# Loads in held-back groups, and a first walk through TensorE's code, in a two-block convolution kernel

## The chip, the cores and the metric

The kernel runs on one core of a Trainium2 chip. The metric is the device time of one execution in microseconds. Times in this text are in us unless marked otherwise. TensorE is the matrix engine (PE in the rows; PEld its weight loads), VectorE is DVE, ScalarE is ACT, GpSimd is POOL and SyncE is SP. A q behind an engine's name in a row (SPq) means its sequencer: DMA issues, branches, waits.

## The reference

The input x has 16 images of 32 channels with 128 x 128 pixels in float32. Two residual blocks follow each other:

```
x = x + conv3x3(group_norm(x, 16 groups), masked L0 weights)
x = x + conv5x5(group_norm(x, 16 groups), L1 weights) + bias
```

The 3x3 weights are masked by a threshold on the mean of their absolute values. The reference writes the 5x5 convolution with Fourier transforms; it equals a direct one with padding 2. A group is two channels of one image, so each normalization needs the mean and variance of whole images.

## The kernel before, in words

**Halves and steps.** Each image is worked on in two halves of 64 rows, 32 halves in all (h). A half is held in two layouts. In x_bands and mid_bands the partitions are 4 bands x 32 channels, each band 16 rows with a halo above and below: this is what the matmuls read. In x_own and mid they are 4 interleaved sets of rows x 32 channels, as the results come out of the matmuls. Float32 accuracy comes from splitting: values and weights are each a float16 high part and a float16 low part, and three of the four products are taken (high x high, high x low, low x high).

**Stages of a half.** load_bands(h) brings x in bands (4 DMAs of 272 to 288 KB), load_own(h) the same rows in the other layout (4 DMAs of 256 KB). VectorE takes statistics of the bands (stats_in, L635). When both halves of an image are done, they are combined over the partitions: for images 0 and 1 of x and image 0 of mid by a small matmul on TensorE (mix_members, L948, and combine on VectorE), later by a round trip through DRAM (spread_stats and gather_stats on ScalarE, group_stats on VectorE). Then scale_of, normalize3 (L709 or ScalarE's L449), high3 (L404, x_hi), low3 (L737, x_lo), the 3x3 convolution on TensorE, take_conv3 (L757: adds x_own and makes mid; its drain at L760 frees the PSUM banks, bank3_go), stats_out (L765), and move_mid(h): 16 DMAs (L273) that bring mid into bands, with move_edges (L280, L284) for the halo rows between halves. The 5x5 convolution of a half comes LAG = 3 steps later, then take_conv5 (L481), the addition on GpSimd (L380) and store_out.

**TensorE's program.** In the lead (halves 0 to 2) a small piece of code, lead_conv, does one 3x3 convolution at a time, with some matmuls on constant data (keep_warm) between. From step 3 on, a loop does in each step the 3x3 convolution of half s and the 5x5 convolution of half s - 3: whole_step (pairs3_high, pairs3_low), conv5 (pairs5_high), conv3_rest (singles3), conv5_rest (singles5, pairs5_low), with a branch at L1004 back to whole_step, which a prefetch hint at L990 goes with. In a step there are 144 + 320 + 144 + 240 + 160 = 1008 matmuls, each with its weight load. whole_step is aligned to 256 instructions. The program starts with a branch (L959) to lead_start, which lies behind lead_conv; there it waits for mix_members(("x", 0)).

**Queues and order.** SyncE issues nearly all DMAs, in program order, in one queue: bands 0, 1 and 2, w5, bands 3, own 0 and 1; then it waits for mid_made (the first take_conv3) and goes on with own 2, move 0, an edge, bands 4, own 3, an edge, bands 5, move 2, bands 6 and 7. Nothing holds one load back until another has landed; SyncE stops only at these waits, or where the queue is full. GpSimd issues move 1 (16 DMAs), with its two operations on w5 (L371 and L374) between them. VectorE's order in the lead is written out by hand (L785 to L833):

```
stats_in(0..1), set_apart(x 0), drain, combine(x 0), scale_of(x 0), normalize3(0), low3(0),
stats_in(2..3), set_apart(x 1), largest(w5), take_conv3(0), low3(1), combine(x 1), scale_of(x 1),
stats_out(0), take_conv3(1), low3(2), over_partitions, power_of_two, undo_power (scale of w5),
stats_out(1), set_apart(mid 0), take_conv3(2), ...
stats_in(6), stats_in(7), group_stats(x 2), scale_of(x 2), normalize3(4), take_conv3(3), ..., low3(4)
```

## Time and profile before

| what | value |
|---|---|
| median of 3 runs | 806.02 us (805.27 to 806.18) |
| the profiled execution | 805.87 us |
| its span | 804.1 us |
| TensorE busy | 748.7 us, 93% |
| VectorE busy | 611.8 us, 76% |
| mean granted TensorE clock | 0.988 |
| DMA | 150.49 MB, mean 187 GB/s |

The profile is of one execution. The span is the time from the first to the last instruction of the core; 1.8 us lie around it. Busy times are the union of an engine's instructions. The share of the DMA engines in the view of stretches is the mean over 16 engines and can exceed 1, as packets on one engine overlap. The idle time in front of an instruction is put down to what ended it; "issue" means nothing that the profile shows. Queue q1 is SyncE's loads and stores; q8 and q14 carry instructions, q8 in packets of 16 KB.

### The profile page before, as it was taken

The page shows a single profiled execution, that of the slowest core. Times are in us where ns is not written, and L with a number is a line of the kernel's source. Part 1 is how long each engine was busy: PE and PEld are TensorE (multiplying, and loading weights), DVE is VectorE, ACT ScalarE, POOL GpSimd, SP SyncE. Part 2 cuts the span into 40 slices and gives each one's busy share as a digit, 9 for nine tenths or more (in the row PEclk, how much of TensorE's full clock was granted, in tenths as well). Part 3 has the DMA queues.
Part 4 walks back from the last instruction along what each step waited for, and adds up shares of the span by engine and source line. Part 5 has one row for each costly group of instructions (what it writes and reads, how often), then busy time and mean ns, then how long its engine had stood idle before and what let it go on. Part 6 is the DMA issues. An engine that isn't in the chain of part 4 may idle for free.

```text
span 804.1 us, 67794 instructions
## 1 busy us (share of the span) xinstructions
PE 748.7 (93%) x32292; PEld 552.8 (69%) x32292; DVE 611.8 (76%) x959; ACT 332.4 (41%) x287; POOL 267.9 (33%) x161
## 2 busy tenths in 40 slices
PE   0786699999999999999999999999999999999996
PEld 0443367777787777877777787777778777776564
DVE  5897598797878788787878788797878796664541
ACT  0351235363534435363444435363444426362410
POOL 1050044432324343432234343422234343322360
PEclk9998999999999999999999999999999999999999
DMA  8999589999998979798998979898998957573424
GB/s 196 194 202 218 130 173 230 222 224 216 228 203 213 221 169 223 180 220 198 229 203 194 229 165 230 183 225 197 225 210 205 199 126 165 133 167 86 103 52 104
DMA packets 234176, 150.49 MB, mean 187 GB/s; under 512 B 18656, under 2 KB 227616, under 8 KB 230048
## 3 DMA queue, kind: packets, MB, share of 16 engines
q1 hardware_dynamic: 227168, 144.00, 81.8%
q10 hardware_dynamic: 6272, 4.90, 2.5%
q0 software_dynamic: 704, 1.25, 0.7%
q14 instruction: 22, 0.18, 0.1%
q8 instruction: 10, 0.16, 0.1%
HBM read 75.60 MB, written 33.59 MB: 136 GB/s over the span
## 4 chain that ended last, share of the span: by engine, by line
PE 86%; DVE 5%; SPq 3%; DMA 3%; issue 1%; DVEq 1%; ACT 1%; ACTq 0%
PE psum L887 66%; PE psum L904 21%; DMA x_bands<-x_dram 3%; SPq L265 1%; SPq L273 1%; DVE bn_in L635 1%; DVE x_lo L737 1%; DVE bn_out L765 1%; DVE mid L757 1%; DVEq L760 1%; SPq L280 0%; ACT conv_out L481 0%; ACT x_hi L411 0%; DVE x_bands L709 0%; DVE mid L868 0%
## 5 line engine op out<-in xcount | busy, mean ns | idle before, releaser
L380 POOL TENSOR_TENSOR mid<-mid,conv_out 128x512 f32<-128x512 f32 x118 | 244.6, 2103 | 471.1 <-ACT conv_out L481 471.1
L887 PE MATMUL psum<-x_hi,s_hi 32*64 32x508 f16 (+2 forms) x6656 | 200.2, 381 | 13.2 <-ACTq L521 4.8
L887 PE MATMUL psum<-x_lo,s_hi 32*64 32x508 f16 (+2 forms) x6656 | 197.6, 379 | 3.8 <-DVE x_lo L737 2.8
L887 PE MATMUL psum<-x_hi,s_lo 32*64 32x508 f16 (+2 forms) x6656 | 198.1, 377 | 0.6 <-issue 0.6
L887 PEld LDWEIGHTS psum<-x_hi,s_hi 32*64 32x64 f16 x6656 | 130.4, 105 | 70.8 <-issue 9.5
L887 PEld LDWEIGHTS psum<-x_hi,s_lo 32*64 32x64 f16 x6656 | 149.7, 104 | 36.3 <-issue 3.5
L887 PEld LDWEIGHTS psum<-x_lo,s_hi 32*64 32x64 f16 x6656 | 108.5, 104 | 78.4 <-issue 9.8
L757 DVE SCALAR_TENSOR_TENSOR mid<-psum,unscale,x_own 128x1024 f32<-128x1024 f32 x64 | 79.2, 1278 | 93.2 <-PE psum L904 93.1
L404 ACT ACTIVATE x_hi<-x_bands 128x2304 f16<-128x2304 f32 x31 | 65.7, 2118 | 116.0 <-PE psum L904 116.0
L481 ACT ACTIVATE conv_out<-psum,bias,unscale 128x512 f32<-128x512 f32 x118 | 82.3, 776 | 60.1 <-PE psum L887 58.7
L745 DVE TENSOR_TENSOR x_lo<-mid_bands,x_hi 128x2560 f16<-128x2560 f32 x32 | 93.5, 2921 | 2.9 <-PE psum L887 2.8
L442 ACT ACTIVATE x_hi<-mid_bands 128x2560 f16<-128x2560 f32 x31 | 72.5, 2338 | 49.9 <-PE psum L904 48.4
L397 ACT ACTIVATE root<-gvar 128x1 f32<-128x1 f32 x32 | 6.5, 203 | 194.0 <-DVE gvar L688 168.7
L635 DVE BATCH_NORM_STATS2 bn_in<-x_bands 128x6 f32<-128x512 f32 x128 | 76.9, 664 | 12.1 <-DMA x_bands<-x_dram 12.1
L449 ACT ACTIVATE mid_bands<-mid_bands,nbias,gscale 128x2560 f32<-128x2560 f32 x31 | 78.2, 2524 | 15.8 <-DVE nbias L702 13.3
L765 DVE BATCH_NORM_STATS2 bn_out<-mid 128x6 f32<-128x512 f32 x128 | 79.1, 681 | 4.4 <-DVE mid L757 0.5
L737 DVE TENSOR_TENSOR x_lo<-x_bands,x_hi 128x2304 f16<-128x2304 f32 x32 | 80.7, 2523 | 1.5 <-ACT x_hi L415 1.1
L904 PE MATMUL psum<-x_hi,s_hi 32*32 32x508 f16 (+2 forms) x4096 | 74.0, 377 | 6.2 <-issue 6.2
L904 PE MATMUL psum<-x_hi,s_lo 32*32 32x508 f16 (+2 forms) x4096 | 73.9, 378 | 0.0
L904 PEld LDWEIGHTS psum<-x_hi,s_hi 32*32 32x32 f16 x4096 | 53.2, 88 | 24.2 <-issue 20.0
L709 DVE TENSOR_SCALAR x_bands<-x_bands,gmean,gscale 128x2304 f32<-128x2304 f32 x29 | 68.8, 2373 | 0.0
L904 PE MATMUL psum<-x_lo,s_hi 32*32 32x508 f16 (+2 forms) x4096 | 67.1, 381 | 0.8 <-issue 0.8
(88 smaller groups left out, 342.6 us busy)
## 6 DMA issues: line engine op xcount, KB each, us to landing
x_own<-x_dram SPq DMA_DIRECT2D x128, 256.0 KB, 4.9
mid_bands<-mid SPq DMA_DIRECT2D x372, 80.0 KB
out_dram<-mid SPq DMA_DIRECT2D x112, 256.0 KB, 5.4
x_bands<-x_dram SPq DMA_DIRECT2D x96, 288.0 KB, 6.0
x_bands<-x_dram SPq DMA_DIRECT2D x32, 272.0 KB, 6.6
mid_bands<-mid SPq DMA_DIRECT2D x124, 64.0 KB
every_mv<-mv_scratch ACTq DMA_DIRECT2D x16, 256.0 KB, 3.9
out_dram<-mid SPq DMA_DIRECT2D x28, 128.0 KB, 2.4
```

The source lines that it names most:

```text
L380: nc.gpsimd.tensor_tensor(m, m, conv_out[:, b, :], ALU.add).then_inc(out_added, 1)
L442: nc.scalar.activation(x5_hi[:, :, 2:2 + W], mid_bands[:, k % MB_SLOTS, :, :], ACT.Copy).then_inc(hi5_done, 1)
L449: nc.scalar.activation(v, v, ACT.Identity, bias=nbias[:, at], scale=gscale[:, at]).then_inc(act_scaled, 1)
L481: nc.scalar.activation(conv_out[:, b, :], psum[:, X5_BANK + b, :], ACT.Identity, bias=bias[:, 0:1], scale=unscale[:, 1:2]).then_inc(conv5_ ...
L635: nc.vector.bn_stats(bn_in[:, h // 2 % 2, h % 2, b, :], rows.rearrange("p a w -> p (a w)")).then_inc(bn_x, 1)
L709: nc.vector.tensor_scalar(v, x_bands[:, h % XB_SLOTS, :, :], gmean[:, 0:1], gscale[:, 0:1], ALU.subtract, ALU.mult).then_inc(scaled, 1)
L737: nc.vector.tensor_tensor(x3_lo[:, :, 2:2 + W], x_bands[:, h % XB_SLOTS if h else SPARE, :, :], x3_hi[:, :, 2:2 + W], ALU.subtract).then_i ...
L745: nc.vector.tensor_tensor(x5_lo[:, :, 2:2 + W], mid_bands[:, k % MB_SLOTS, :, :], x5_hi[:, :, 2:2 + W], ALU.subtract).then_inc(x5_lo_go, 1)
L757: nc.vector.scalar_tensor_tensor(mid[:, h % MID_SLOTS, at, :], psum[:, X3_BANK + at.start:X3_BANK + at.stop, :], unscale[:, 0:1], x_own[:, ...
L765: nc.vector.bn_stats(bn_out[:, h % 2, b, :], mid[:, h % MID_SLOTS, b, :]).then_inc(bn_mid, 1)
L887: ins = nc.tensor.matmul(psum[2 * C * J:2 * C * (J + 1), bank + i, :].rearrange("p (a w) -> p a w", a=A)[:, :, c0:c1], w[quad(i), at:at + ...
L904: ins = nc.tensor.matmul(psum[quad(j), bank + i, :].rearrange("p (a w) -> p a w", a=A)[:, :, c0:c1], w[quad(i), at, :], src[quad(i), j + d ...
```

## The change

Four things change.

1. load_own and load_bands take a semaphore and a count. With them, the group's first DMA is issued, and the other three only when that semaphore says that the group before has landed. It is used from the second group on for all loads of the lead up to bands 7. w5 is loaded before bands 2 instead of behind them.
2. VectorE takes the largest of w5 before combine(("x", 0)), and computes its scale between normalize3(0) and low3(0).
3. GpSimd does its two operations on w5 before move 1, and ScalarE makes s5_hi (high_w5) behind high3(1) instead of high3(3).
4. TensorE's program starts with a branch to fetch_second, and from there to fetch_third and fetch_fourth. Each of these stubs is a nop and a branch, and lies between parts of the loop's code: behind whole_step, behind the first half of pairs5_high, and within its second half. The fourth branch goes to lead_start. The parts of the loop are joined by three branches (whole_step to conv5, conv5 to conv5_more, conv5_more to conv5_last); their matmuls and their order are the same.

The diff, cut to its core:

```diff
         @block.sync
-            def load_own(h):
+            def load_own(h, behind=None, count=0):
                 for j in range(Q):
+                    if behind is not None and j == 1:
+                        sp.wait_ge(behind, 16 * count)
                     sp.dma_start(as_rows(x_own, j, h % X_SLOTS), own_rows(x[h // 2], h % 2, j),
                                  ).then_inc(x_own_in[h % X_SLOTS], 16)
...
             load_bands(0)
-            load_bands(1)
-            load_bands(2)
+            load_bands(1, x_bands_in[0], Q)
             for q in range(Q):
                 sp.dma_start(w5[quad(q), :, :], w5_dram.rearrange("i a b o -> i (a b) o")).then_inc(w_loaded, 16)
-            load_bands(3)
-            load_own(0)
-            load_own(1)
+            load_bands(2, x_bands_in[1], Q)
+            load_bands(3, x_bands_in[2], Q)
+            load_own(0, x_bands_in[3], Q)
+            load_own(1, x_own_in[0], Q)
             sp.wait_ge(mid_made, PIECES)
-            load_own(2)
+            load_own(2, x_own_in[1], Q)
             move_mid(0)
             move_edges(0, 1, 0)
-            load_bands(4)
-            load_own(3)
+            load_bands(4, mid_bands_in[0], MOVES)
+            load_own(3, x_bands_in[4], Q)
             move_edges(0, 0, 1)
-            load_bands(5)
+            load_bands(5, x_own_in[1], 2 * Q)
             move_mid(2)
-            load_bands(6)
-            load_bands(7)
+            load_bands(6, mid_bands_in[2], Q * Q)
+            load_bands(7, x_bands_in[0], 2 * Q)
...
         @block.gpsimd
+            pool.wait_ge(w5_bounded, 1)
+            nc.gpsimd.tensor_scalar(w5[:, :, :], w5[:, :, :], wfac[:, 1:2], None, ALU.mult).then_inc(w5_scaled, 1)
+            pool.wait_ge(w5_hi_made, 1)
+            nc.gpsimd.tensor_tensor(s5_lo[:, :, :], w5[:, :, :], s5_hi[:, :, :], ALU.subtract).then_inc(w5_split, 1)
             pool.wait_ge(mid_made, PIECES * 2)
...
         @block.vector
             set_apart("x", 0)
+            dve.wait_ge(w_loaded, 16 * Q)
+            largest(w5, 1)
             dve.drain().then_inc(bank3_go, 1)
...
             normalize3(0)
+            over_partitions(total[:, 1:2], bound[:, 1:2])
+            power_of_two(1)
+            undo_power(1)
             low3(0)
+            nc.vector.drain().then_inc(w5_bounded, 1)
...
         @block.tensor
-            pe.br("lead_start")
+            pe.br("fetch_second")
...
             with nc.body("whole_step", valid_engines=only):
                 hint = pe.mark_branch_hint_location()
                 pairs3_high()
                 pairs3_low()
+                pe.br("conv5")
+            with nc.body("fetch_second", valid_engines=only):
+                pe.nop().then_inc(code_touched, 1)
+                pe.br("fetch_third")
             with nc.body("conv5", valid_engines=only):
-                pairs5_high()
+                pe.wait_ge(x5_hi_go, 1)
+                pairs(s5_hi, x5_hi, K5, X5_BANK, start=True, every=x5_hi_go)
+                pe.br("conv5_more")
+            with nc.body("fetch_third", valid_engines=only):
+                pe.nop().then_inc(code_touched, 1)
+                pe.br("fetch_fourth")
+            with nc.body("conv5_more", valid_engines=only):
+                pairs(s5_lo, x5_hi, K5, X5_BANK, part=slice(0, 3))
+                pe.br("conv5_last")
+            with nc.body("fetch_fourth", valid_engines=only):
+                pe.nop().then_inc(code_touched, 1)
+                pe.br("lead_start")
+            with nc.body("conv5_last", valid_engines=only):
+                pairs(s5_lo, x5_hi, K5, X5_BANK, part=slice(3, K5))
                 pe.br_lt(step, HALVES, on_true="conv3_rest", on_false="conv5_rest")
```

## Rows read from the trace of the kernel before

**Rows 1.** The page, part 4: the chain that ended last, by engine.
```profile
PE 86%; DVE 5%; SPq 3%; DMA 3%; issue 1%; DVEq 1%; ACT 1%; ACTq 0%
```

**Rows 2.** Stretches: length; busy (count) by engine; TensorE's clock; DMA share; GB/s.
```profile
110.00:795.00 685.00, 679.80 (x30112) 514.20 (x30104) 525.38 (x786) 299.38 (x259) 246.02 (x118) 1.00 0.85 188
...
2.00:36.00 34.00, 12.64 (x310) 7.24 (x310) 24.08 (x62) 9.05 (x8) 2.47 (x10) 1.00 1.05 216
36.00:38.00 2.00, 0.50 (x16) 0.27 (x24) 1.80 (x3) 0.00 (x0) 0.00 (x0) 0.73 0.10 18
...
50.00:90.00 40.00, 26.77 (x834) 14.23 (x819) 28.08 (x54) 6.43 (x6) 11.75 (x16) 0.85 1.06 218
```

**Rows 3.** The chain in order of time, 80 to 107: start, length, what.
```profile
80.00 0.42 SPq L265
...
80.47 10.50 DMA x_bands<-x_dram
...
90.99 2.48 DVE bn_in L635 x4
...
96.39 1.48 DVE x_bands L709
...
99.27 1.20 DVEq L760
...
103.71 2.42 DVE x_lo L737
```

**Rows 4.** Waits up to 110: total, times, longest.
```profile
PE psum L904 <- issue: 7.0, 3, 4.8
...
PE psum L887 <- issue: 4.8, 3, 3.2
```

**Rows 5.** Timeline of TensorE and ScalarE: start, length, instruction, [idle before].
```profile
64.55 2.79 PE L887 MATMUL psum<-x_lo,s_hi 32*64 32x512 f16 x48 [2.38 <-DVE x_lo L737]
...
73.79 2.55 PE L887 MATMUL psum<-x_hi,s_hi 32*64 32x504 f16 x51 [3.16 <-issue]
...
98.27 2.12 ACT L404 ACTIVATE x_hi<-x_bands 128x2304 f16<-128x2304 f32 x1
...
102.75 1.67 PE L887 MATMUL psum<-x_hi,s_hi 32*64 32x512 f16 x48
...
106.18 1.53 PE L887 MATMUL psum<-x_lo,s_hi 32*64 32x512 f16 x48 [0.43 <-DVE x_lo L737]
```

**Rows 6.** Line 959; queue q8 in the 0.1 us from 1.8, 9.0 and 70.8.
```profile
L959 PEldq COMPARE_BRANCH  x1: 3695/3695/3695, 0.9 to 0.9; - x1
...
q8 instruction: 1, 0.02, 78.3%
...
q8 instruction: 1, 0.02, 77.4%
...
q8 instruction: 1, 0.02, 83.8%
```

**Rows 7.** Timeline of TensorE and VectorE, 20 to 37.
```profile
20.02 0.58 PE L948 MATMUL psum<-apart,mix_in 128*128 128x16 f32 x2 [20.02 <-DVE apart L657]
...
20.64 0.17 DVE L663 COPY members<-psum 128x16 f32<-128x16 f32 x1 [0.76 <-PE psum L948]
...
25.88 2.56 DVE L737 TENSOR_TENSOR x_lo<-x_bands,x_hi 128x2304 f16<-128x2304 f32 x1 [1.07 <-ACT x_hi L415]
...
33.91 0.98 DVE L586 TENSOR_REDUCE bound<-w 128x1 f32<-128x800 f32 x1
...
34.92 2.48 DVE L757 SCALAR_TENSOR_TENSOR mid<-psum,unscale,x_own 128x1024 f32<-128x1024 f32 x2
```

**Rows 8.** DMA issues of 5.9 to 6.2 and 30.3 to 30.8; SyncE's timeline.
```profile
x_bands<-x_dram SPq DMA_DIRECT2D x1, 272.0 KB, 10.7
...
x_own<-x_dram SPq DMA_DIRECT2D x2, 256.0 KB, 7.1
...
37.43 1.91 SPq L254 DMA_DIRECT2D x_own<-x_dram  x4
39.38 10.43 SPq L273 DMA_DIRECT2D mid_bands<-mid  x16
```

**Rows 9.** VectorE's timeline: first and last of the eight steps of w5's scale.
```profile
50.51 0.17 DVE L579 COPY across<-bound 128x32 f32<-128x32 f32 x1
...
51.94 0.15 DVE L601 TENSOR_SCALAR unscale<-power 128x1 f32<-128x1 f32 x1
```

**Rows 10.** Line 1004, the loop's branch: duration in ns, min/median/max.
```profile
L1004 PEldq COMPARE_BRANCH  x32: 71/217/240, 102.2 to 795.7; - x32
```

More of the change, by code:

```diff
@@ L148, in two_blocks @@
         apart_go = sem("apart_go")
+        code_touched = sem("code_touched")
         c3_whole = sem("c3_whole")
@@ L260, in store_out, with load_bands @@
                                  as_rows(mid, j, k % MID_SLOTS, banks)).then_inc(out_stored[k % MID_SLOTS], 16)
-            def load_bands(h):
+            def load_bands(h, behind=None, count=0):
                 for i in range(Q):
+                    if behind is not None and i == 1:
+                        sp.wait_ge(behind, 16 * count)
                     y0, y1, at = band(h % 2, i, 1)
@@ L368, in _ @@
                     pool.dma_start(to, rows).then_inc(mid1_moved, 16)
-                if i == 1:
-                    pool.wait_ge(w5_bounded, 1)
-                    nc.gpsimd.tensor_scalar(w5[:, :, :], w5[:, :, :], wfac[:, 1:2], None, ALU.mult).then_inc(w5_scaled, 1)
-                elif i == 2:
-                    pool.wait_ge(w5_hi_made, 1)
-                    nc.gpsimd.tensor_tensor(s5_lo[:, :, :], w5[:, :, :], s5_hi[:, :, :], ALU.subtract).then_inc(w5_split, 1)
             def add_out(k, b):
@@ L529, in _ @@
                     high3(1)
+                    high_w5()
                     take_root(("x", 1))
@@ L536, in _ @@
                     high3(3)
-                    high_w5()
                     take_root(("mid", 0))
@@ L797, in _ @@
             set_apart("x", 1)
-            dve.wait_ge(w_loaded, 16 * Q)
-            largest(w5, 1)
             take_conv3(0)
@@ L806, in _ @@
             low3(2)
-            over_partitions(total[:, 1:2], bound[:, 1:2])
-            power_of_two(1)
-            undo_power(1)
-            nc.vector.drain().then_inc(w5_bounded, 1)
             stats_out(1)
@@ L872, in _, with columns, pairs @@
         def _(pe):
-            def columns(k):
-                for dx in sorted(range(k), key=lambda d: abs(d - k // 2)):
+            def columns(k, part=slice(None)):
+                for dx in sorted(range(k), key=lambda d: abs(d - k // 2))[part]:
                     x0 = 2 - k // 2 + dx
                     yield dx, x0, max(0, 2 - x0), min(W, W + 2 - x0)
-            def pairs(w, src, k, bank, start=False, every=None):
-                for dx, x0, c0, c1 in columns(k):
+            def pairs(w, src, k, bank, start=False, every=None, part=slice(None)):
+                for dx, x0, c0, c1 in columns(k, part):
                     for dy in range(1, k):
@@ L926, in singles3 @@
                 singles(s3_hi, x3_lo, K3, X3_BANK).then_inc(c3_whole, 1)
-            def pairs5_high():
-                pe.wait_ge(x5_hi_go, 1)
-                pairs(s5_hi, x5_hi, K5, X5_BANK, start=True, every=x5_hi_go)
-                pairs(s5_lo, x5_hi, K5, X5_BANK)
             def singles5():
@@ L985, in _ @@
                 pe.br("lead_end")
-            nc.switch_bb("lead_end")
-            pe.addr_align(256, offset=0, max_nops=0)
-            pe.br("whole_step")
+            with nc.body("lead_end", valid_engines=only):
+                pe.addr_align(256, offset=0, max_nops=0)
+                pe.br("whole_step")
             with nc.body("whole_step", valid_engines=only):
```

## The prediction

> **What bounds the kernel now.** I read the page's chain first, for the engine that sets the end: TensorE [rows 1]. The view of stretches then says where time can be won. From 110 to 795 us TensorE is busy for 679.8 of 685 us [rows 2], so nothing can be gained there, and whatever happens in the lead (the first 106 us) is carried to the end one for one. In the lead the DMA engines are the full resource: 216 GB/s from 2 to 36 us and 218 GB/s from 50 to 90 us, their share above 1 in both [rows 2].
>
> The chain over the end of the lead [rows 3] is what the change has to beat. The last piece of load_bands(7), issued at 80.47, lands at 90.97. VectorE takes its statistics until 93.46, and only then, its program being in order, the group statistics of image 2, normalize3(4) at 96.39, take_conv3(3), stats_out(3) and low3(4), which ends at 106.13. TensorE begins pairs3_low(4) at 106.18, after 0.43 us of waiting for it [rows 5].
>
> Next the waits. TensorE loses 4.8 + 7.0 = 11.8 us before L887 and L904 to "issue" in this time [rows 4], all of it in its first pass over whole_step to conv5_rest, between 70 and 100 us. The instruction queue explains them: one q8 packet between 70.8 and 70.9, and TensorE goes on at 73.79 [rows 5, 6]. TensorE is fetching code that it has not yet run.
>
> **The change, part by part.** (a) *Code fetched ahead.* In whole_step and the bodies after it are 1008 matmuls with their loads (2016 instructions) and some ten others. The stubs touch its second to fourth parts. They take away the first of the stalls, at most the 11.8 us. But if step 3 ended 11.8 us sooner (before it ends at 102.75 [rows 5]), TensorE would stand before step 4: its x_hi, made by high3(4) behind the same statistics, comes at 98.27 + 2.12 = 100.4 [rows 5], bank3_go, the end of the drain at L760, at 100.47 and x_lo at 106.13 [rows 3]. The gain is 0.43 us, the wait now left, and not 11.8. What ends last there is the transfer of bands 7.
>
> The Trainium skill speaks against this part too (Runtime: NRT & Kernel Launch, "Instruction fetch mechanics": the instruction memory is a FIFO, "only 2 cache lines", and a taken branch outside it forces a fetch). By that rule the stubs' blocks would be gone before their use, and every jump back of the loop would fetch. The trace disagrees for TensorE: the branch that closes the loop, L1004, runs 32 times at a median of 0.217 us and at most 0.240 [rows 10], where a fetch cost 3.70 [rows 6]. So I count the stubs' blocks as kept; as (a) is worth 0.43 us at most, the sum is the same by either.
>
> (b) *What the stubs cost.* One jump to code that is not there takes 3.70 us, from 0.90 to 4.60, with nearly empty queues: 0.95 us to the packet at 1.85, and 2.75 from there to running [rows 6] (2.94 at 70.85 [rows 5, 6]). On arrival the next block is asked for; that packet starts only at 9.05, 4.45 us later, since the loads are under way by then [rows 6]. After the change TensorE needs four such trips in a row before lead_start instead of one. First to 4.60. Second: packet at 9.05, running at 11.8. Third: the packet starts between 0.95 and 4.45 us after 11.8, running at 15.5 to 19.0. Fourth, back to lead_start: 19.2 to 26.2, and if it stands behind the packet of the block after the fourth stub, up to some 28. I take delays near the loaded one for both, 3.8 and 4.0, as the rest of bands 1 and then w5 fill the queues at just that time: third at 18.3, lead_start at 25.0. It is needed at 20.02, for the mix of x 0 [rows 7]. **TensorE is 5.0 us late**, bounds 0 and 8. Behind that mix waits combine(("x", 0)) on VectorE (20.64, idle only 0.76 before it [rows 7]) and with it everything. A late mix gives nothing back: VectorE's queue is full until take_conv3(0) at 34.92.
>
> (c) *w5's work on VectorE.* largest (0.98 us [rows 7]) moves to before combine(x 0), where the wait of (b) covers it; without that cover it costs 0.3. It waits for w5, which now stands before bands 2: 0.4 MB at 216 GB/s behind bands 1 (16.6) land near 18.5 to 19, not late. The scale's eight small steps (50.51 to 52.09 [rows 9]: 1.6 us) go between normalize3(0) and low3(0). There VectorE was idle for 1.07 us [rows 7], so 0.6 us lie on the path. largest's old place before take_conv3(0) gives 0.98 back. Sum -0.3 on the path to take_conv3(0). The steps leave the path to take_conv3(2), which comes 1 to 2.5 us earlier; nothing that ends last hangs on it, as SyncE is still issuing older work when bands 6 and 7 are due. GpSimd's two w5 operations now go ahead of move 1, and its 16 moves without gaps; hidden.
>
> (d) *Held-back loads to take_conv3(0).* Each group's first DMA goes, and the rest waits until the group before has landed. From the landing to the first bytes of the rest pass an issue (0.42 us [rows 3]) and a start-up, which I set equal to the 0.95 us of (b): about 1.4 us. The DMA already queued covers 288 KB / 216 GB/s = 1.35 us of it, less where the 16 engines end apart: a pause of 0 to 0.6 us for each change of group. Bands 1's last DMA (issued 5.91, 10.7 us later landed [rows 8]) comes 0 to 0.6 later, own 1 (its last DMA is issued at 30.4, 7.1 to its landing: 37.5 [rows 8]) about 1 later. That is before the end of the new take_conv3(0), so own 1 costs nothing when TensorE is late; if it is not, about 0.5. Behind each waiting DMA on SyncE stand only the later loads, and, until mid_made, no move.
>
> So take_conv3(0) ends 5.0 - 0.3 = 4.7 later, and SyncE's wait for mid_made, behind which all later loads stand, too.
>
> (e) *Held-back loads from there to bands 7.* Before: SyncE goes on at 37.43 [rows 8], so 90.97 - 37.4 = 53.6 us. After, counted from that point: own 2 and move 0 as before (16 issues in 10.43 us [rows 8], set by SyncE), edges until 13.7. Bands 4's rest waits for the edges to land (15.3), then 1.2 start-up, 3 x 1.35 for itself and 2.2 for the moves of GpSimd beside it, 0.5 to the last landing: 23. Own 3's rest likewise 28.6 (no moves beside it), bands 5's 34.5. Move 2 is issued until 30.0 + 10.4 = 40.4 and has landed near 42.2; bands 6 near 48.1; bands 7's rest, behind which SyncE holds nothing urgent, 48.2 + 1.4 + 4.05 + 0.5 = 54.2. Until bands 7, what waits behind each held load on SyncE is the next of these, and the edges 0 to 1 and move 2, which nobody misses before step 4. **+0.6 us**, bounds -4.4 and +4. The lower bound is the 49.2 us that the bytes of own 2 and 3, bands 4 to 7 and three moves take with no pause (their DMAs at 1.2, 1.35 and 0.35 us each), the upper one four bare pauses of 1 us. The skill gives a fixed 2 us for each DMA (DMA: Bandwidth & Descriptors, "Anatomy of one DMA"), most of it after the last byte; by it each of four groups would pause for 2.0 - 1.35 = 0.65, together 2.6 instead of 0.6, and the sum would be 813.8.
>
> (f) *Clock.* TensorE will now stand idle for some microseconds before step 4. After 2.38 us of idle time its next 48 matmuls took 2.79 us instead of 1.53 [rows 5], the level of 1.2 GHz. pairs3_high(4) is then slow but hidden by the wait for x_lo; pairs3_low(4) may be slow: 0 or 1.3, I take 0.6.
>
> (g) *Three more branches in every step.* L1004 costs 0.217 us in the sequencer and the matmuls around it keep their pace [rows 5, 10]: they are queued ahead. Nothing; 0.1 us each if the cover were gone, 29 x 3 x 0.1 = 8.7.
>
> Sum: 4.7 + 0.6 + 0.6 - 0 = **+5.9 us**. The profiled execution took 805.87 us (span 804.1), the median is 806.02: 811.8 us.
>
> **The rivals.**
> *No late start, slower by little.* The held-back groups leave the queues emptier, the trips take 3.7 us each, lead_start is reached at 19.2. For it: the first trip. Against: the second, with only seven band loads issued (after: five). Left are (c) 0.3, (d) 0.5, (e) 0.6, (f) 0.6: 808.0.
> *Faster.* Short queues let each transfer run without a pause, and take the place of SyncE's long stalls in a full queue; bands 7 land 4.4 us sooner, with no late start. For it: there are pauses now, e.g. 36 to 38 us. Against: 218 GB/s over 40 us leave little. It decides if the packet of the third trip starts by 13.5 us and bands 7 land before 89: 806.0 - 4.4 + 1.0 = 802.6.
> *No difference.* Half of either: 806.
> *The branches are not hidden*: 811.8 + 8.7 = 820.5.
>
> **How the numbers follow.** Forecast 0.53 (own range 808.5 to 815.5, a TensorE late by 2 to 8 us); little slower 0.18, of which 0.10 over 0.2%; no difference 0.10; faster 0.14; branches 0.05. A measurement of this kernel tells 0.2%, 1.6 us. Faster 0.14, same 0.18, slower 0.68. The range leaves out the branches and most of faster: 804 to 817.
>
> **What would show it.** TensorE's first matmul (L948) at 25 instead of 20.02, and its branch instructions before it at 3 to 7 us each. Four q8 packets or more before 25 us. take_conv3(0) at 39.6 instead of 34.92. The stalls at 73.79, 79.73 and 87.90 gone, a wait for normalize3(4)'s or bank3_go's chain of 6 us or more in their place before step 4. Bands 7 landed near 96. From step 5 on steps as long as before. I am wrong if L948 stays at 20 (step (b)), if bands 7 land earlier than 90 ((e)), or if steady steps are longer ((g)).

## The result and the profile after

The changed kernel takes 817.97 us (median of 5, 816.34 to 820.3), the kernel before 805.97 us beside it (5, 805.23 to 806.18). The ratio is 1.0142, interval 1.0127 to 1.0158: slower by 12.0 us. The profiled execution took 816.34 us with a span of 814.5, 10.4 more than before. It is the shortest of the five, so the trace accounts for 10.4 us and leaves some 1.5 us of the medians' difference unseen. Of the runs further down, one execution of f2 took 1129.72 us at a mean granted clock of 0.657, where all others have 0.97 to 0.99; it is left out of the ratio, and without it the median of f2 is 807.09.

First the chain that ended last, by engine, from the page of the profile; [rows 1] has it for the kernel before.

```profile
PE 84%; DMA 8%; SPq 4%; DVE 2%; issue 1%; ACT 0%; DVEq 0%; ACTq 0%
```

The DMA engines' part of the chain went from 3% to 8%. The view of stretches says where the time is lost. A row has the stretch, its length, the busy time (and count) of the five engines, TensorE's granted clock, the DMA share and GB/s.

```profile
2.00:36.00 34.00, 12.52 (x304) 6.62 (x304) 23.35 (x66) 8.42 (x8) 4.76 (x11) 1.00 0.84 193
50.00:90.00 40.00, 32.03 (x1181) 19.30 (x1166) 24.48 (x42) 7.58 (x6) 8.93 (x16) 0.87 0.82 180
...
73.10:85.30 12.20, 8.36 (x416) 5.80 (x416) 5.17 (x9) 0.00 (x0) 0.00 (x0) 0.87 0.75 153
...
110.00:795.00 685.00, 678.59 (x29848) 496.36 (x29856) 535.85 (x795) 305.57 (x265) 251.56 (x119) 1.00 0.85 188
```

Behind the lead nothing changed: from the end of x_lo(4) to the end of the span are 697.7 us, before 698.0. In the lead, where [rows 2] had 216 and 218 GB/s, there are now 193 and 180, and in the 12.2 us from 73.1 on only 153 (the stretch in which SyncE issues move 2). The chain in order of time shows what the DMA engines wait for (start, length, what).

```profile
17.01 0.31 SPq L270
...
17.83 6.85 DMA x_bands<-x_dram
...
24.69 0.31 SPq L270
...
25.51 5.22 DMA x_bands<-x_dram
...
31.67 4.97 DMA x_own<-x_dram
...
37.55 4.80 DMA x_own<-x_dram
...
42.36 0.31 SPq L257
...
60.23 5.41 DMA x_bands<-x_dram
...
66.56 5.20 DMA x_own<-x_dram
...
90.18 5.40 DMA x_bands<-x_dram
...
96.42 5.30 DMA x_bands<-x_dram
101.74 2.47 DVE bn_in L639 x4
...
107.04 1.48 DVE x_bands L713
...
114.36 2.42 DVE x_lo L741
```

It is one pattern again and again: a group of loads lands, SyncE issues the rest of the next group (0.8 us from the landing to the end of the second issue), that group lands, and so on. Own 1 has landed at 42.35 instead of 37.52, bands 7 at 101.72 instead of 90.97, and x_lo(4) ends at 116.78 instead of 106.13. SyncE's timeline has the step between these (its first issue of each kind, the time that the group of issues takes, and their number):

```profile
42.36 1.38 SPq L257 DMA_DIRECT2D x_own<-x_dram  x3
43.79 10.63 SPq L278 DMA_DIRECT2D mid_bands<-mid  x16
...
60.70 6.35 SPq L257 DMA_DIRECT2D x_own<-x_dram  x4
...
68.28 4.75 SPq L270 DMA_DIRECT2D x_bands<-x_dram  x4
73.08 12.23 SPq L278 DMA_DIRECT2D mid_bands<-mid  x16
```

take_conv3(0) ended at 39.45, and SyncE then issued the first DMA of own 2; but own 2's second DMA waits for own 1, so that SyncE gets no further until 42.36. In the kernel before it went on at 37.43 [rows 8]. Move 2 is issued from 73.08; in the kernel before, SyncE came to it at 63.40:

```profile
60.43 2.93 SPq L265 DMA_DIRECT2D x_bands<-x_dram  x4
63.40 12.27 SPq L273 DMA_DIRECT2D mid_bands<-mid  x16
```

TensorE's branches in the lead, by line (duration in ns, min/median/max, first and last start), and its timeline:

```profile
L957 PEldq COMPARE_BRANCH  x1: 3810/3810/3810, 0.9 to 0.9; - x1
...
L994 PEldq COMPARE_BRANCH  x1: 6294/6294/6294, 4.9 to 4.9; - x1
...
L1002 PEldq COMPARE_BRANCH  x1: 4847/4847/4847, 11.4 to 11.4; - x1
...
L1008 PEldq COMPARE_BRANCH  x1: 5566/5566/5566, 16.6 to 16.6; - x1
...
L1019 PEldq COMPARE_BRANCH  x32: 82/228/3673, 93.7 to 806.1; - x32
```

```profile
22.28 0.58 PE L946 MATMUL psum<-apart,mix_in 128*128 128x16 f32 x2 [22.28 <-issue]
...
80.94 1.07 PE L908 MATMUL psum<-x_lo,s_hi 32*32 32x508 f16 x56 [2.53 <-issue]
...
84.97 0.62 PE L908 MATMUL psum<-x_hi,s_hi 32*32 32x504 f16 x8 [1.31 <-issue]
...
91.04 3.63 PE L891 MATMUL psum<-x_lo,s_hi 32*64 32x508 f16 x121 [1.50 <-issue]
111.22 2.79 PE L891 MATMUL psum<-x_hi,s_hi 32*64 32x512 f16 x48 [16.56 <-DVEq L764]
...
116.83 1.53 PE L891 MATMUL psum<-x_lo,s_hi 32*64 32x512 f16 x48 [0.37 <-DVE x_lo L741]
```

The four trips through the stubs took 20.5 us in all. The first mix comes 2.26 us later than in [rows 7]. Of the 11.8 us of stalls "issue" of [rows 4], 5.3 us are left (the three rows from 80.94 to 91.04), and in their place stand 16.56 us before step 4.

### The profile page after: what moved, and what is told of

Read it like the earlier page. It is cut to its first block, busy times and chain, and to the rows that moved or that the text cites. A ratio compares the mean times of both kernels' runs of the same rounds, so it can differ in the third digit from the quotient of the medians.

```text
span 814.5 us, 67893 instructions
## 1 busy us (share of the span) xinstructions
PE 749.9 (92%) x32292; PEld 537.9 (66%) x32292; DVE 610.6 (75%) x959; ACT 332.4 (41%) x287; POOL 268.5 (33%) x161
## 4 chain that ended last, share of the span: by engine, by line
PE 84%; DMA 8%; SPq 4%; DVE 2%; issue 1%; ACT 0%; DVEq 0%; ACTq 0%
PE psum L891 64%; PE psum L908 20%; DMA x_bands<-x_dram 5%; SPq L278 3%; DMA x_own<-x_dram 2%; DMA mid_bands<-mid 1%; SPq L270 1%; SPq L257 0%; DVE bn_out L769 0%; DVE bn_in L639 0%; DVE x_lo L741 0%; ACT conv_out L485 0%; DVE x_bands L713 0%; DVE mid L872 0%; DVEq L764 0%
## 5 line engine op out<-in xcount | busy, mean ns | idle before, releaser
L891 PEld LDWEIGHTS psum<-x_hi,s_hi 32*64 32x64 f16 x6656 | 124.4, 105 | 88.2 <-DVEq L764 21.8
L891 PEld LDWEIGHTS psum<-x_hi,s_lo 32*64 32x64 f16 x6656 | 141.7, 104 | 42.6 <-issue 1.4
L891 PEld LDWEIGHTS psum<-x_lo,s_hi 32*64 32x64 f16 x6656 | 107.0, 104 | 80.9 <-issue 10.4
```

The costliest lines, as they stand in the source:

```text
L891: ins = nc.tensor.matmul(psum[2 * C * J:2 * C * (J + 1), bank + i, :].rearrange("p (a w) -> p a w", a=A)[:, :, c0:c1], w[quad(i), at:at + ...
```

## The experiments

Go-on is the time from which SyncE is free to go on with own 2: mid_made, or own 1's landing where own 2 is held for it and that is later. Two lengths then describe every run's lead: from go-on to the first issue of move 2, and from there to the landing of bands 7. "Early waits" are those of bands 1 to own 1, "late waits" those from own 2 on.

| kernel | median us (runs) | ratio, interval | go-on | move 2 issued | bands 7 landed | x_lo(4) ends |
|---|---|---|---|---|---|---|
| before | 805.97 (5) | 1 | 37.4 | 63.40 | 90.97 | 106.12 |
| after | 817.97 (5) | 1.0142, 1.0127 to 1.0158 | 42.36 | 73.08 | 101.72 | 116.78 |
| e1_stubs_only | 817.2 (4) | 1.0128, 1.0111 to 1.0146 | 48.30 | 73.79 | 102.32 | 117.39 |
| e2_held_only | 815.83 (4) | 1.0109, 1.0092 to 1.0127 | 40.87 | 72.95 | 103.72 | 118.77 |
| e3_no_stubs | 817.43 (4) | 1.0138, 1.0118 to 1.0158 | 41.09 | 72.73 | 102.32 | 117.37 |
| e4_no_hold | 815.98 (4) | 1.0115, 1.0098 to 1.0132 | 47.23 | 73.83 | 101.37 | 116.59 |
| e5_two_ahead | 815.29 (4) | 1.0116, 1.0099 to 1.0132 | 39.84 | 71.08 | 98.82 | 113.88 |
| e6_hold_early | 808.65 (6) | 1.0041, 1.0022 to 1.0059 | 40.18 | 66.41 | 92.25 | 107.32 |
| e7_late_hold_no_stubs | 814.55 (4) | 1.0093, 1.007 to 1.0117 | 37.25 | 70.40 | 101.30 | 116.35 |
| e8_no_move_hold | 816.38 (4) | 1.0131, 1.011 to 1.0153 | 43.37 | 74.03 | 102.11 | 117.17 |
| f1_hold_before_move2 | 812.68 (5) | 1.0083, 1.007 to 1.0096 | 37.09 | 70.87 | 98.45 | 113.52 |
| f2_hold_bands7 | 807.18 (12) | 1.0015, 1.0005 to 1.0025 | 38.76 | 64.47 | 95.69 | 110.78 |

Times in the last four columns are of one profiled execution each, ratios of all. The profiled executions of e2 and f2 lie 2.4 and 2.6 us above their medians, those of e5 and e6 2.2 and 1.4 below. Without late waits before move 2, from go-on to move 2 are 25.5 to 26.6 us (before, e1, e4, e6, f2); with them 30.7 to 33.8 (after, e2, e3, e5, e7, e8, f1). From move 2 to bands 7 are 25.8 to 31.2 in all.

**Stubs and waits apart.** The first two put each half of the change into the kernel before, the next two take each out of the kernel after.

e1: the kernel before with the whole TensorE program of after, stubs and parts as in the diff of the change.

```diff
+        code_touched = sem("code_touched")
...
-            pe.br("lead_start")
+            pe.br("fetch_second")
```

> The kernel before with TensorE's stubs and split bodies alone; loads and w5 as before. Theory P (pauses): the held-back groups cost the 12 us, the stubs nothing in the changed kernel, because own 1 lands at 42.35 there, behind the end of take_conv3(0). Alone, with all loads posted at once, the trips are slower: 3.7, 7, 7 and 7 us, lead_start near 24.5, L948 4 to 5 us late, and as here nothing hides it, 810 to 811 us. Theory T (the trips are the cost): L948 as in the changed kernel, 22.3, and nearly all of the 12 us: 816 to 818.

Slower by 1.28%, nearly as much as the whole change. The branches and SyncE's go-on:

```profile
L954 PEldq COMPARE_BRANCH  x1: 3830/3830/3830, 0.9 to 0.9; - x1
...
L991 PEldq COMPARE_BRANCH  x1: 6534/6534/6534, 4.9 to 4.9; - x1
...
L999 PEldq COMPARE_BRANCH  x1: 8747/8747/8747, 11.7 to 11.7; - x1
...
L1005 PEldq COMPARE_BRANCH  x1: 9997/9997/9997, 20.7 to 20.7; - x1
```

```profile
48.30 1.91 SPq L255 DMA_DIRECT2D x_own<-x_dram  x4
```

With nothing held back, the third and fourth trips take 8.7 and 10.0 us instead of 4.8 and 5.6. The first mix comes at 30.87, 10.85 late, take_conv3(0) ends 10.87 late, and x_lo(4) is 11.27 late. This is step (b)'s mechanism at twice its 5.0, over its bound of 8. The time is the one that theory T named, but not its way: I expected the first mix at 22.3.

e2: the kernel before with all waits, and none of the other edits.

```diff
+                    if behind is not None and j == 1:
+                        sp.wait_ge(behind, 16 * count)
...
-            load_own(1)
+            load_own(1, x_own_in[0], Q)
             sp.wait_ge(mid_made, PIECES)
-            load_own(2)
+            load_own(2, x_own_in[1], Q)
```

> The kernel before with the waits between the groups of loads alone; w5 behind bands 2 as before, no stubs. Theory P: each change of group pauses the queues by about 1 us, own 1 lands near 42.3, bands 7 near 101.5 instead of 90.97, 816 to 818 us. Theory T: 806 to 808.

Slower by 1.09%, just under the 816 to 818 us of theory P. The first mix is on time (19.50), own 1 lands 3.35 later than in the kernel before, and from there to bands 7 are 62.9 us, where the prediction had 54.2.

e3: after, with the first branch straight to lead_start.

```diff
-            pe.br("fetch_second")
+            pe.br("lead_start")
```

> The changed kernel, its first branch going straight to lead_start; all code stays where it is. Theory P: L948 back at 20.0, take_conv3(0) about 2 us earlier, but own 1 and bands 7 as in the changed kernel (42.3, 101.7); the stalls between 70 and 90 come back and are paid from the 16.6 us wait before step 4: 817 to 818 us. Theory T: 806 to 812.

1.38% against 1.42%: taking the stubs out gives nothing. The mix comes at 19.81, take_conv3(0) ends at 37.74, but own 1 lands at 41.09, and own 2's wait stands for it. TensorE's late start in the kernel after was covered. This is as theory P had it.

e4: after, without any of the waits.

```diff
-            load_own(1, x_own_in[0], Q)
+            load_own(1)
             sp.wait_ge(mid_made, PIECES)
-            load_own(2, x_own_in[1], Q)
+            load_own(2)
```

> The changed kernel with all waits between groups taken out; order of loads, w5's early work and the stubs stay. Theory P: own 1 near 37.5, bands 7 near 91 plus what L948 is late; with full queues the trips last longer, L948 at 24 to 25, 809 to 811 us. If the trips are as short as in the changed kernel (22.3), 808. Theory T: 818.

1.15%, and the picture of e1: trips of 6.35, 8.09 and 10.0 us, the mix at 30.04. Theory P (809 to 811 us) had this run wrong. Each half alone costs 9 to 11 us (e2 and e3, e1 and e4) and both together 11 to 12: the costs don't add, because with the early waits the trips are shorter (the mix at 22.28 and not 30), and because the two delays lie side by side up to own 2.

**Which waits.** e5 lets two DMAs of each group go ahead of its wait.

```diff
-                    if behind is not None and j == 1:
+                    if behind is not None and j == 2:
```

> The changed kernel, but in each group two DMAs go ahead of the wait instead of one. If the loss is the pause between the landing of a group and the first bytes of the next one's rest (theory P), a second queued DMA of 1.3 us covers it: own 1 near 39.5 instead of 42.35, bands 7 near 95 instead of 101.7, 810 to 812 us; L948 a little later than 22.3. If the loss is elsewhere (theory S: the waits of SyncE delay small moves behind them, not the queue's pause), bands 7 stay near 101: 816 to 818.

1.16% against 1.42%. Own 1 landed at 39.15 instead of 42.35, so the bare pauses are mostly filled; but from go-on to move 2 are still 31.2 us. Filling the pauses takes away some 2 us at most (the intervals touch), and not the cost. Theory P (810 to 812 us) is refuted by this run, and bands 7 at 98.8 came sooner than theory S had them.

e6 keeps the early waits and the stubs, and takes the late waits out.

```diff
-            load_own(2, x_own_in[1], Q)
+            load_own(2)
...
-            load_bands(4, mid_bands_in[0], MOVES)
-            load_own(3, x_bands_in[4], Q)
+            load_bands(4)
+            load_own(3)
...
-            load_bands(5, x_own_in[1], 2 * Q)
+            load_bands(5)
...
-            load_bands(6, mid_bands_in[2], Q * Q)
-            load_bands(7, x_bands_in[0], 2 * Q)
+            load_bands(6)
+            load_bands(7)
```

> The changed kernel with the waits up to own 1 alone; own 2 and everything behind it as before. Theory P: own 1 near 42.3 and L948 near 22.3 as in the changed kernel, from there 53.6 us to bands 7 as before: near 94.5, 809 to 811 us. Theory S the same.

0.41%: of the 12 us only 2 to 3.3 are left (808.65 against 806.60 of the kernel before beside it; 3.3 by the ratio). The trips were 3.80, 6.87, 5.11 and 5.41 us, the mix at 22.95. SyncE's timeline:

```profile
60.31 4.02 SPq L285 DMA_DIRECT2D mid_bands<-mid  x2
64.37 1.99 SPq L270 DMA_DIRECT2D x_bands<-x_dram  x4
66.41 10.75 SPq L278 DMA_DIRECT2D mid_bands<-mid  x16
```

Both theories had expected more, 809 to 811 us. Bands 5 are issued in 1.99 us, at once; move 2 begins 6.7 us sooner than in the kernel after, and bands 7 land 9.5 us sooner.

e7 is the opposite: no early waits and no walk through the stubs, the late waits in. The work on w5 and the three branches of the loop stay as in the kernel after.

```diff
-            pe.br("fetch_second")
+            pe.br("lead_start")
...
-            load_own(1, x_own_in[0], Q)
+            load_own(1)
```

> The changed kernel with the waits from own 2 on alone, and no stubs. Early part as before: L948 at 20, take_conv3(0) ends near 37.6, own 1 near 37.5. Theory P: bands 7 take the changed kernel's 59.4 to 61 us from there: 97 to 98.5, 813 to 814 us.

0.93%, with the mix at 19.82 and go-on at 37.25 as before. With the late waits bands 7 land 10.3 us later than in the kernel before, 2.8 us later than theory P's upper end of 98.5; that profiled execution (815.85) lies above its median of 814.55.

e8 is after without the two waits on moves.

```diff
-            load_bands(4, mid_bands_in[0], MOVES)
+            load_bands(4)
...
-            load_bands(6, mid_bands_in[2], Q * Q)
+            load_bands(6)
```

> The changed kernel without the two waits that hang on moves (bands 4 on move 0, bands 6 on move 2). In the changed kernel the rest of bands 4 goes 2.95 us and the rest of bands 6 3.5 us after it could. Theory P: both are saved in part, bands 7 near 97, 812 to 814 us. If the transfers were queued behind the moves anyway, nothing: 817 to 818.

1.31% against 1.42%, the intervals overlap: these two waits cost nothing that shows, where theory P had 4 us and more. Of the waits behind go-on, it is then own 3's, bands 5's or bands 7's. (Own 2's makes go-on itself later, where own 1 lands late; in e7 own 1 had landed by then, so it cost nothing there.)

**The two that delay move 2, and the one behind it.** f1 puts only the waits of own 3 and bands 5 into the kernel before, f2 only that of bands 7.

```diff
-            load_own(3)
+            load_own(3, x_bands_in[4], Q)
...
-            load_bands(5)
+            load_bands(5, x_own_in[1], 2 * Q)
```

> The kernel before with two of the waits alone: own 3 behind bands 4, bands 5 behind own 3. Theory S (SyncE stands in waits, so move 2, whose 16 issues take 10 to 12 us one by one, starts late, and the queues then run short of work): move 2 begins near 70 instead of 63.4, bands 7 land 5 to 7 us later, 811 to 813 us. Theory P (each wait costs its own pause of about 1 us and no more): bands 7 2 us later, 808.

```diff
-            load_bands(7)
+            load_bands(7, x_bands_in[0], 2 * Q)
```

> The kernel before with one wait alone: bands 7 behind bands 6. No move stands behind it. Theories S and P agree: one pause, bands 7 about 1 to 1.5 us later, 807 to 808 us. If a held load were free, 806.

f1 costs 0.83%, 6.7 us: more than half of the whole change, from two waits. SyncE's timeline in f1, and there the stretch of move 2's issues:

```profile
52.88 9.50 SPq L256 DMA_DIRECT2D x_own<-x_dram  x4
...
63.67 7.15 SPq L269 DMA_DIRECT2D x_bands<-x_dram  x4
70.87 13.65 SPq L277 DMA_DIRECT2D mid_bands<-mid  x16
```

```profile
70.90:84.50 13.60, 9.71 (x404) 5.57 (x389) 7.40 (x13) 0.00 (x0) 0.00 (x0) 1.00 0.70 156
```

The same stretch, of move 2's issues, in the kernel before, and below it in e6:

```profile
63.40:75.60 12.20, 7.89 (x205) 4.03 (x213) 9.64 (x11) 1.59 (x2) 0.00 (x0) 0.81 1.12 216
```

```profile
66.40:77.10 10.70, 10.70 (x376) 5.81 (x362) 7.86 (x11) 0.00 (x0) 0.00 (x0) 0.89 1.14 219
```

As theory S had it, move 2 begins 7.5 us later than in the kernel before, and bands 7 land 7.5 us later. The loads ahead of it are hardly late: the last DMA of own 3 lands at 69.17 (before 68.99), that of bands 5 at 75.32 (before 74.12). While its 16 issues of 64 to 80 KB run, 156 GB/s flow where the kernel before has 216 and e6 219. When the issues begin in the kernel before, bands 5 still take 10.7 us to land (63.40 to 74.12; in e6 8.7), and their bytes flow during the issues; in f1 it is 4.5 us (70.87 to 75.32). So the moves, which used to be issued while the loads flowed, now come behind them. f2 costs 0.15%, 1.2 us in the medians' ratio. Its trace has bands 7 4.7 us later, but there the mix was 1.35 late as well, which that edit doesn't touch; the ratio is the better measure.

A kernel with these two waits and with bands 6 and 7 ahead of move 2 would test the account directly. It was not run.

**What would be won if bands 7 came sooner?** The change means to take TensorE's stalls away; step (a) says that this is worth nothing while bands 7 end last. g1 issues bands 6 and 7 ahead of move 2 in the kernel before, g2 does the same in e6.

```diff
-            move_mid(2)
             load_bands(6)
             load_bands(7)
+            move_mid(2)
```

> The kernel before with bands 6 and 7 issued ahead of move 2 instead of behind it; nothing else. If the landing of bands 7 is the gate of step 4, as my prediction has it, it goes from 91 to about 83, and the gate becomes the gather of the statistics or TensorE's own step 3 (102.7, less what its code fetches gain from emptier queues): 800 to 805 us. If that landing is not the gate: 806, or slower because move 2 is later.

> The kernel of e6 (stubs, early w5, waits up to own 1) with bands 6 and 7 issued ahead of move 2. If the gate is gone, the code that the stubs brought can count: step 3 ends near 97, 800 to 804 us. If the late start of L948 (22.9) decides, no better than e6 less 1: 807.

g1 took 806.58 us (11 executions), ratio 1.0006 (0.9997 to 1.0015), and g2 806.13 (12), 1.0022 (1.0003 to 1.0041). I had expected 800 to 805 and 800 to 804. In g1 bands 7 land at 85.31, 5.7 us sooner, x_lo(4) ends at 104.68, and yet nothing is won: TensorE's timeline now has its own stalls last.

```profile
97.21 0.39 PE L904 MATMUL psum<-x_hi,s_hi 32*32 32x504 f16 x4 [1.47 <-issue]
...
100.61 3.47 PE L887 MATMUL psum<-x_lo,s_hi 32*64 32x508 f16 x116 [0.47 <-issue]
103.75 1.67 PE L887 MATMUL psum<-x_hi,s_hi 32*64 32x512 f16 x48
```

Step 3 ends at 103.75, stretched by 12.7 us of stalls "issue". So two gates stand side by side before step 4: bands 7 with the statistics behind them, and the code. In the kernel before they are 0.43 us apart [rows 5]. In g2, with the stubs, step 3 ends at 101.12, though two stalls "issue" of 6.47 and 3.62 us are left in it, and TensorE waits 1.73 us for x_lo(4), which ends at 105.66: the exchange of statistics (issued at 86.41, its root at 94.72) is the next gate.

g3 and g4 open that too. SyncE waits for the gathered statistics before it issues bands 6 and 7 and then move 2, and VectorE takes the statistics of bands 6 and 7 only behind low3(4): g3 in e6, g4 in the kernel before.

```diff
-            move_mid(2)
+            sp.wait_ge(mv_in, 16)
             load_bands(6)
             load_bands(7)
+            move_mid(2)
...
-            stats_in(2 * LAG, range(BANKS))
-            stats_in(2 * LAG + 1, range(BANKS))
...
             stats_out(LAG)
+            low3(LAG + 1)
+            stats_in(2 * LAG, range(BANKS))
+            stats_in(2 * LAG + 1, range(BANKS))
             aggregate("mid", LAG // 2)
             aggregate("x", LAG, mv_ready)
-            low3(LAG + 1)
```

> The kernel of e6 (stubs, early w5, waits up to own 1) with three moves: SyncE waits for the gather of image 2's statistics, then issues bands 6 and 7, then move 2; VectorE takes the statistics of halves 6 and 7 behind low3(4). By my theory of the gate: gather landed near 83 instead of 92, x_lo(4) near 95, step 3 of TensorE ends near 98 with its first blocks fetched ahead, step 4's 5x5 part waits for ScalarE until about 104 instead of 107.5: 802 to 804 us. If the fetched code and the gate don't matter: 806 to 809.

> The kernel before with the same three moves as g3, without stubs and waits between groups. The gate goes as in g3; TensorE's step 3 still fetches its code block by block, though with emptier queues (2.5 us a block instead of up to 4.8), and ends near 100: 802 to 804 us. g3 is better than g4 only if its fetched code saves more than the 2 to 3 us by which its first matmul is late.

g4, without stubs, took 806.28 us (11), ratio 1.0007 (0.9997 to 1.0017), where I had expected 802 to 804. x_lo(4) ends at 95.11, 11 us sooner, and TensorE still begins step 4 at 104.24, behind 13.2 us of stalls:

```profile
94.76 0.61 PE L905 MATMUL psum<-x_hi,s_hi 32*32 32x504 f16 x4 [6.40 <-issue]
...
104.24 1.66 PE L888 MATMUL psum<-x_hi,s_hi 32*64 32x512 f16 x48
```

g3, with stubs and early waits, took 804.6 us (12), ratio 0.9983 (0.9967 to 0.9999). It is the only kernel whose interval lies below 1, and it hardly does. Against g4 it is 1.7 us faster by the medians, which fits the fetched code being worth something once its gate decides; the two differ in the early waits and w5's work as well, so this is not shown for the stubs alone, nor is it seen in the trace. The profiled execution of g3 (807.35 us, its mix as late as 26.45) begins step 4 at 99.44, behind a stall of its own:

```profile
99.44 2.79 PE L892 MATMUL psum<-x_hi,s_hi 32*64 32x512 f16 x48 [4.38 <-issue]
```

The branch back to whole_step took 5.08 us there in its first run. In the nine kernels that don't make the trips (before, e2, e3, e7, f1, f2, g1, g4, g6) that first run took 0.24, in the nine that do 0.7 to 5.7.

g5 and g6 are g3 and g4 with the next exchange of statistics behind take_conv5(0), for which step 4's 5x5 part waited 2.15 us in g3.

```diff
-                if s == LAG:
+                if s in (LAG, LAG + 1):
                     spread_stats(s - 1)
...
-                if exchanged(s) and s >= LAG:
+                if exchanged(s) and s > LAG:
                     spread_stats(s)
```

> g3, and ScalarE takes the results of the first 5x5 convolution (take_conv5(0)) before it sends off the statistics of step 3, and not behind them. The wait of step 4's 5x5 part goes: another 1 to 2 us, 800 to 803.

> g4 with ScalarE's order as in g5: 801 to 804 us; by 1 to 2 better than g4 if TensorE would reach the 5x5 part of step 4 before ScalarE has sent the statistics, else equal.

g5 took 805.29 us (12), ratio 0.9995 (0.9977 to 1.0012), and g6 806.54 (12), 1.0009 (0.9997 to 1.002): no gain, where I had expected 800 to 804. In g5 the wait of 2.15 us is gone and step 4's 5x5 part begins at 102.20, but TensorE stood for 4.96 us before step 4, behind a first branch back of 5.66. Its step 4 ends at 120.57 and that of the kernel before at 125.85 (the ends of the loop's branch); three steps later 1.5 us of these 5.3 are left (193.29 against 194.82), since its steps 5 and 7 take 24.7 and 24.8 us, where a steady one takes 22.7. Why they are longer was not followed.

## Why the prediction was wrong

Its sign and its gate (bands 7 end last) were right, its size was not: +5.9 forecast, +10.4 in the trace, +12.0 in the medians. At 817.97 the time lies beyond the range of 804 to 817. The step that failed is (e), "Held-back loads from there to bands 7": +0.6 forecast, +5.8 measured. Besides, (b) was sized too large and (d) too small, and it is (d) and not (b) that makes SyncE late; that the two came out alike is luck.

(a) *Code fetched ahead*: right. Of 11.8 us of stalls 6.5 went, and nothing came of it; x_lo(4) ended last, as said. The 0.43 us of [rows 5] has another side, which I had not put down: it is also about all that a sooner landing of bands 7 is worth alone, as g1 and g4 show.

(b) *What the stubs cost*: the mechanism right, the term mis-sized. The trips after the first were forecast at 7.2, 6.5 and 6.7 us with a full queue, and measured at 6.29, 4.85 and 5.57; the mix was 2.26 late instead of 5.0. I had read the delay from a queue with nothing held back, and with the early waits less is in it. Where nothing is held back, e1, I was as far off to the other side: 8.7 and 10.0 us, the mix 10.85 late, over my bound of 8. In the kernel after, this term decides nothing (e3), as (d) covers it.

(c) *w5's work on VectorE*: -0.3 forecast, -0.21 measured (take_conv3(0) ends 2.05 later behind a mix 2.26 later).

(d) *Held-back loads to take_conv3(0)*: 0 to 0.6 us for each change of group, own 1 about 1 later. Measured: own 1 4.83 later over five held groups, 1.0 each; without the trips 3.35 and 3.57 (e2, e3), 0.7 each. And I had own 1 cost nothing because it would land before the end of take_conv3(0). But it landed 2.9 behind it, and own 2's second DMA waits for own 1, and with it SyncE's whole program. Go-on is 42.36, 4.9 late: by size near the 4.7 that I had for another reason. The Trainium skill (DMA: Bandwidth & Descriptors, "Anatomy of one DMA") gives a fixed 2 us for a DMA, in a section on those that GpSimd issues, where these are SyncE's. By it I had estimated a pause of 0.65; the traces have 0.7 to 1.0, so that rule was nearer than my 0 to 0.6.

(e) *Held-back loads from there to bands 7*: the step that failed. Forecast +0.6, measured 101.72 - 42.36 = 59.4 against 53.6, +5.8, over the upper bound of 4. By its own marks, counted from go-on:

| | forecast | measured |
|---|---|---|
| bands 4 landed | 23 | 23.3 |
| own 3 landed | 28.6 | 29.4 |
| bands 5 landed | 34.5 | 35.7 |
| move 2 issued until | 40.4 | 43.0 |
| move 2 landed | 42.2 | 46.9 |
| bands 6 landed | 48.1 | 53.2 |
| bands 7 landed | 54.2 | 59.4 |

Up to bands 5 the sum held within 1.2 us. Then it breaks, at move 2. I took for its 16 issues the 10.4 us of move 0 [rows 8], where the kernel before already needs 12.27 for those of move 2, and I had it landed 1.8 behind the last of them, where it took 4.0. I wrote that behind each held load on SyncE stands only the next, "and the edges 0 to 1 and move 2, which nobody misses before step 4". Nobody misses move 2's data; but bands 6 and 7 are issued behind its 16 issues.

Against the kernel before, 4.7 of the 5.8 stand ahead of move 2 (issued from 30.7 after go-on, before from 26.0) and 1.1 behind it (28.6 to bands 7, before 27.6). The loads themselves are not what is late: bands 5 have landed 35.7 after go-on, before 36.7. What is gone is the overlap. In the kernel before the end of own 3 and bands 5 flow while move 2 is issued (landed at 68.99 and 74.12); held back, SyncE issues their rest only when own 3 has landed, and comes to move 2 when little of them is left. Then small DMAs (1.2 MB in all) flow for 12.2 us with little beside them: 153 GB/s, where the kernel before has 216. By an estimate from these rows, the missing 63 GB/s x 12.2 us = 0.77 MB are 3.6 us at 216 GB/s; the rest are the pauses of the held groups. f1 shows the same with these two waits alone (+6.7 us, 156 GB/s), e6 by their absence. I had counted bytes and pauses, and not who issues the bytes. f2 adds 1.2 us for the wait of bands 7. Bands 6's rest did wait for move 2 (landed at 89.30), but without the waits on moves (e8) bands 7 come only 0.6 sooner, counted from go-on. The lower bound of this step was also summed wrongly: its own terms (8 x 1.2, 16 x 1.35, 48 x 0.35) give 48.0 and not 49.2, and the rival "faster" took its 4.4 us from it.

(f) *Clock*: forecast 0.6, nothing measured. TensorE's first 48 matmuls behind the 16.56 us of idle time took 2.79 us at a granted clock of 0.50 (1.2 GHz), and the next 48 2.68, under the cover of the wait for x_lo; pairs3_low took 1.53 at a granted clock of 1.00 (2.4 GHz).

(g) *Three more branches in every step*: nothing, as said. From x_lo(4) to the end are 697.7 us against 698.0, and the 24 steps from 8 to 31 take 545.8 against 545.2. The loop's branch has a median of 0.228 us. Only its first run took 3.67, from 93.69, and a q8 packet starts in it, at 94.72: a block of the loop had to be fetched once more. TensorE waited behind it anyway, but in g3 and g5 it shows. I had not put this down.

Of the rivals, "faster" (short queues run without a pause) fell with e2 and e7, both slower by 0.9% and more with no late mix; the gain that it wanted at the start is real only for the instruction fetches (e6 against e1). What I had named as signs came true in kind (four branches of 3 to 7 us, six q8 packets before 25 us, a wait of over 6 us before step 4, steps as long as before) and not in size: the first mix came at 22.28 and not 25, take_conv3(0) began at 36.99 and not 39.6, bands 7 landed at 101.7 and not 96. The stalls of step 3 were to be gone; three of six are left, with 5.3 of 11.8 us.

4.9 (own 1) + 5.8 (own 3, bands 5, bands 7) = 10.7 at the landing of bands 7, against 10.4 of the span. Still open: the 1.5 us between the trace and the medians; and why the kernel after costs 0.3% more with its own edits (e3) than the waits alone (e2), where the intervals overlap.

## What to carry to other kernels

A wait on a queue that one sequencer fills in program order costs more than the pause that it makes, namely the backlog that it takes away: look for the next long row of small issues behind it, and ask what the DMA engines will have to do in that time. Count separately when the bytes could flow and when they are issued, and let the later one decide. Before paying for something that removes a stall, take the work that ends last away first (as g1 does): only then can the stall's removal show what it is worth. And look whether what was fetched ahead pushes the cost to another place (here the first branch back of the loop).

## What the runs showed of the hardware

- **A fetch of code waits with the data.** The first trip, with nearly empty queues, takes 3.7 to 4.0 us in all runs. The third and fourth take 4.8 and 5.6 us with loads held back to about one group (3.9 to 6.0 and 5.4 to 8.2 over all such runs), and 8.1 to 8.7 and 10.0 us with nothing held back (e4, e1). In the middle of the lead the longest stall for code was 4.8 us [rows 4], and 6.40 us with bands 7 on their way (g4). The Trainium skill calls the cost of crossing a block "mostly hidden" (Runtime: NRT & Kernel Launch, "Instruction fetch mechanics"); here it isn't in the first pass: 11.8 us of stalls [rows 4].
- **TensorE keeps the loop.** In the kernel after, q8 has no packet between 94.7 and 766 us, while the loop of 1008 matmuls with their loads runs through 28 times. The stubs' blocks, touched before 23 us, are still there after 70: behind 25 us there are four packets, from 78.1 to 94.7, where the kernel before has seven, from 61.7 to 97.3, and the stall of 3.16 us at 73.79 [rows 5] is gone.
- **Its first way back is dearer after the trips.** The first run of the loop's branch takes 0.24 us in the nine kernels that go straight to lead_start, also where the code is laid out as in the kernel after (e3, e7), and 0.7 to 5.7 us in the nine that make the trips. Which block is missing then, and why, no run shows.
- **The pause between held groups** with one DMA of 256 to 288 KB ahead is 0.7 us each without the trips (e2, e3) and 1.0 to 1.2 with them (after, e6, e8); with two ahead (e5) own 1 is 1.6 us late over five groups instead of 4.8.
- **Issues of moves** between SBUF buffers take SyncE 0.60 to 0.65 us each, loads of bands 0.42 and of own 0.49: 16 moves of 64 to 80 KB in 10.4 to 13.9 us are 90 to 120 GB/s, about half of the 216 to 219 that flowed with a backlog of loads.
